# Two graph layers on one core: the x loads, the warm-up, the copies of the opening and ScalarE's order of work are changed

## What is computed

```python
a = adj.astype(x.dtype)
deg = jnp.sum(a, axis=1, keepdims=True)
y = jnp.concatenate([a @ x / deg, x], axis=1) @ weight + bias    # layer 0
x = layernorm(x + y)
h = x @ W.T                                                     # layer 1
e = (h @ a1)[:, None] + (h @ a2)[None, :]
e = jnp.where(adj == 0, -inf, e)
x = layernorm(x + softmax(e, axis=1) @ h)
```

## Time and profile before

| what | value |
|---|---|
| median of 3 runs | 1068.37 us (1066.5 to 1072.28) |
| profiled execution, its own time | 1068.0 us |
| its span, first to last instruction | 1066.3 us |
| mean granted clock of PE | 0.983 of full |
| PE busy | 1002.8 us (94% of the span) |
| ScalarE busy | 598.4 us (56%) |
| VectorE busy | 669.3 us (63%) |
| gathers (q0) | 36864 packets, 268.45 MB, 256 transfers |
| packed store | 1024 KB in each of the first three groups |

### The profile page before, as it was taken

One profiled execution on the slowest core, in us unless ns is written; L12 is line 12 of the kernel. 1 busy time (PEld: TensorE's weight loads), 2 busy tenths in 40 slices (PEclk: granted clock), 3 DMA queues, 4 the chain that ended last, 5 costly groups with the idle time before them and its releaser, 6 DMA issues.

```text
span 1066.3 us, 21633 instructions
## 1 busy us (share of the span) xinstructions
PE 1002.8 (94%) x8769; PEld 873.2 (82%) x8769; DVE 669.3 (63%) x1591; ACT 598.4 (56%) x512; POOL 251.4 (24%) x269
## 2 busy tenths in 40 slices
PE   6787888989899999999999999999999999999996
PEld 6676766878778888888888888888888888888885
DVE  2565667677766867668666675656544656656654
ACT  3887789878788787867767676756421110000000
POOL 2333333333324333333333222222000000000000
PEclk9899988999999999999999999999999999999998
DMA  9799999999999999999999999988330012222011
GB/s 299 283 410 417 423 412 412 410 396 410 407 411 398 419 416 413 397 389 391 386 373 371 359 344 346 338 326 324 122 127 11 32 55 85 85 85 84 16 40 33
DMA packets 51654, 305.33 MB, mean 286 GB/s; under 512 B 6624, under 2 KB 7904, under 8 KB 18016
## 3 DMA queue, kind: packets, MB, share of 16 engines
q0 software_dynamic: 36864, 268.45, 63.7%
q1 hardware_dynamic: 12704, 33.06, 8.8%
q10 hardware_dynamic: 1984, 2.39, 0.8%
HBM read 286.29 MB, written 17.59 MB: 285 GB/s over the span
## 4 chain that ended last, share of the span: by engine, by line
PE 70%; ACT 12%; DMA 9%; issue 5%; DVE 2%; POOL 1%; ACTq 1%; DVEq 0%
PE ps_agg L345 40%; PE ps_part L345 23%; ACT edges L512 9%; DMA adj_in<-in_adj_dram,chunk 8%; PE ps_y L345 4%; DMA bias<-in_L_gnn_bias_dram 1%; DVE edgesT L853 1%; PE ps_h L699 1%; POOL adj_in L1261 1%; ACT L528 1%; ACT L533 1%; PE ps_y L639 1%; ACT edges L542 0%; ACTq L477 0%; PE ps_x1T L692 0%
## 5 line engine op out<-in xcount | busy, mean ns | idle before, releaser
L345 PE MATMUL ps_agg<-parts,edgesT 128*128 128x257 f16 (+1 forms) x5312 | 621.6, 277 | 42.3 <-DVE edgesT L853 42.2
L345 PEld LDWEIGHTS ps_agg<-parts,edgesT 128*128 128x128 fp8e4 x5312 | 523.7, 99 | 128.0 <-DVE edgesT L853 47.6
L512 ACT ACTIVATE edges<-adj_in 128x4096 fp8e4<-128x4096 int32 x126 | 454.6, 3609 | 33.6 <-DMA adj_in<-in_adj_dram,chunk 33.5
L1261 POOL DMA_INDIRECT adj_in<-in_adj_dram,chunk x256 | 249.9, 976 | 496.3 <-ACT edges L512 422.7
L853 DVE STREAM_TRANSPOSE edgesT<-edges 128x512 uint32<-128x512 uint32 x256 | 166.8, 689 | 141.8 <-ACT edges L512 137.5
L345 PE MATMUL ps_part<-parts,edgesT 128*128 128x258 f16 x1664 | 194.6, 273 | 0.0
L345 PEld LDWEIGHTS ps_part<-parts,edgesT 128*128 128x128 fp8e4 x1664 | 162.7, 98 | 22.7
L586 ACT ACTIVATE std<-mean_var,eps 128x1 f32<-128x1 f32 x64 | 18.9, 295 | 204.5 <-DVE mean_var L1090 204.5
L882 DVE SCALAR_TENSOR_TENSOR packed<-edgesT,packed 128x2048 uint32<-128x2048 uint32 x48 | 109.5, 2282 | 0.0
L345 PE MATMUL ps_part<-parts,packed 128*128 128x258 f16 x836 | 96.4, 273 | 0.0
L518 ACT ACTIVATE x1T<-ps_x1T 128x128 f32<-128x128 f32 x64 | 17.6, 275 | 138.6 <-PE ps_x1T L692 138.6
(11 more groups left out here) (116 smaller groups left out, 595.1 us busy)
## 6 DMA issues: line engine op xcount, KB each, us to landing
adj_in<-in_adj_dram,chunk POOLq DMA_INDIRECT x256, 9.0
out_dram<-edges SPq DMA_DIRECT2D x60, 64.0 KB, 2.9
partial_sums<-partial SPq DMA_DIRECT2D x13, 258.0 KB, 7.3
adj_in<-partial_sums SPq DMA_DIRECT2D x13, 258.0 KB, 6.0
packed_adj<-packed SPq DMA_DIRECT2D x3, 1024.0 KB, 9.3
adj_in<-packed_adj SPq DMA_DIRECT2D x2, 1024.0 KB, 6.6
x_all<-in_x_dram SPq DMA_DIRECT2D x6, 256.0 KB, 8.7
x_all<-in_x_dram ACTq DMA_DIRECT2D x6, 256.0 KB, 10.3
```

The source lines that it names most:

```text
L345: done = eng.matmul(bank[:, 0:cols], rows[:, n // BYTES, n % BYTES, :], moving[:, n, :], start=(n == first), stop=(n == last))
L512: act.activation(edges[:, half, :, :], adj_in[:, n % SLOTS, :, :], ACT.Copy, scale=EDGE[t % GROUP], saturate=False).then_inc(s_conv, 1)
L1261: pool.indirect_dma_start(adj_in[:, n % SLOTS, r, :], None, adj_chunks, bass.IndirectOffsetOnAxis(chunk[:, 0:1], 0), element_offset=first_ ...
```

## The change

- GpSimd makes the identity first, then issues the loads of x's partitions 64 to 127 (with their own semaphores `s_xp`), then the chunk numbers; the gathers no longer wait for x. SyncE's queue gets the bias, w1 and a2 behind its x loads. ScalarE's queue keeps only the first piece of x and w0.
- PE transposes the identity into `ps_small` six times before group 0 and eight times before group 1 (`WARM`).
- VectorE copies the transposed x of odd groups (`copy_odd_xT`), ScalarE that of even ones; the four first conversions come after steps 10, 12, 14 and 16.
- `late_group(t)` is t + 1 for t = 1 to 14.
- In ScalarE's step, `convert(t + 1, 0)` comes first, then the late copy, then the x1T copy.

```diff
-        FIRST_AFTER = [11, 13, 15, 16]
+        FIRST_AFTER = [10, 12, 14, 16]
+        WARM = [6, 8]
...
-            j = (t + 3) // 2
-            return j if t % 2 == 1 and AHEAD <= j < GROUPS else None
+            return t + 1 if AHEAD <= t + 1 < GROUPS else None
...
+            sp.dma_start(bias[:, :], b0.rearrange("(o f) -> o f", o=1).to_broadcast([P, F])).then_inc(s_bias, 16)
+            sp.dma_start(w1_sb[:, :], w1).then_inc(s_const1, 16)
+            sp.dma_start(a2_sb[:, :], a1[F:2 * F].rearrange("(p o) -> p o", o=1)).then_inc(s_const1, 16)
...
-            for s in range(QUARTERS):
-                for a in (2, 3):
-                    first = 1 if s == 0 else 0
-                    act.dma_start(x_all[QUAD * a:QUAD * (a + 1), QBLK * s + BYTES * first:QBLK * (s + 1), :]
-                                  .rearrange("p (b c) f -> p b (c f)", c=BYTES), x_quarters[s, a][:, first:, :])\
-                        .then_inc(s_x[s], 16)
...
-            def copy_xT(j):
+            def copy_even_xT(j):
                 act.wait_ge(s_xT, j + 1)
-                if 0 <= j - 2 < AHEAD:
-                    act.wait_ge(s_v, j - 1)
                 wait(act, s_u, j - 1)
-                act.activation(xT[:, j % 2, :, :].rearrange("p c i -> p (c i)"), ps_xT[j % 2][:, :], ACT.Copy)\
-                    .then_inc(s_xTc, 1)
+                if j == 2:
+                    act.wait_ge(s_v, 1)
+                act.activation(xT[:, 0, :, :].rearrange("p c i -> p (c i)"), ps_xT[0][:, :], ACT.Copy)\
+                    .then_inc(s_xTc[0], 1)
...
             for t in range(TILES + 3):
+                if on(t + 1, 0):
+                    convert(t + 1, 0)
+                if late_group(t) is not None:
+                    copy_late_xT(late_group(t))
                 if on(t, 3):
                     copy_x1T(t - 3)
-                if late_group(t) is not None:
-                    copy_late_xT(late_group(t))
                 for g in range(GROUPS - 1):
                     if t == weighted_at(g):
                         weighted_hi(g)
-                if on(t + 1, 0):
-                    convert(t + 1, 0)
...
-                    pe.wait_ge(s_x[j // QUARTERS], 16 * NQ)
-                wait(pe, s_xTc, j - 1)
+                    pe.wait_ge(s_x[j // QUARTERS], 16 * 2)
+                    pe.wait_ge(s_xp[j // QUARTERS], 16 * 2)
+                wait(pe, s_xTc[j % 2], j // 2)
...
+                for _ in range(WARM[j] if j < len(WARM) else 0):
+                    pe.transpose(ps_small[:, 0:P], ident[:, :], ident[:, :])
...
+            def copy_odd_xT(j):
+                dve.wait_ge(s_xT, j + 1)
+                wait(dve, s_u, j - 1)
+                if j == 3:
+                    dve.wait_ge(s_v, 2)
+                dve.tensor_copy(xT[:, 1, :, :].rearrange("p c i -> p (c i)"), ps_xT[1][:, :]).then_inc(s_xTc[1], 1)
...
             for j in range(GROUPS + 1):
+                if j < GROUPS and j % 2 == 1:
+                    copy_odd_xT(j)
                 if j > 0:
                     split_u_lo(j - 1)
...
+            for s in range(QUARTERS):
+                for a in (2, 3):
+                    first = 1 if s == 0 else 0
+                    pool.dma_start(x_all[QUAD * a:QUAD * (a + 1), QBLK * s + BYTES * first:QBLK * (s + 1), :]
+                                   .rearrange("p (b c) f -> p b (c f)", c=BYTES), x_quarters[s, a][:, first:, :])\
+                        .then_inc(s_xp[s], 16)
...
-            pool.wait_ge(s_x[2], 16 * NQ)
             for n in range(2 * TILES):
                 load_half(n)
```

More of the change, by code:

```diff
@@ L199, in bass_two_graph_layers @@
         g_banks = [ps_agg[1], ps_small]
-        s_x = [sem(f"x_landed{s}") for s in range(QUARTERS)]
+        s_x = [sem(f"x_upper_landed{s}") for s in range(QUARTERS)]
+        s_xp = [sem(f"x_lower_landed{s}") for s in range(QUARTERS)]
         s_xfirst = sem("x_first_words_landed")
@@ L233, in bass_two_graph_layers @@
         s_xT = sem("xT_done")
-        s_xTc = sem("xT_copied")
+        s_xTc = [sem("even_xT_copied"), sem("odd_xT_copied")]
         s_u = sem("u_done")
@@ L546, in _ @@
             for j in range(GROUPS + 1):
-                if j < GROUPS:
-                    copy_xT(j)
+                if j < GROUPS and j % 2 == 0:
+                    copy_even_xT(j)
                 if j > 0:
@@ L635, in dense @@
             def dense(j):
-                pe.wait_ge(s_xTc, j + 1)
+                pe.wait_ge(s_xTc[j % 2], j // 2 + 1)
                 wait(pe, s_lo0, j - 1)
@@ L1244, in _ @@
         def _(pool):
[L1245 to L1248, removed]
             pool.memset(ident[:, :], 0.0).then_inc(s_id, 1)
@@ L1255, in _ @@
                                pattern=[[-1, P]], channel_multiplier=1).then_inc(s_fill, 1)
+            for s in range(QUARTERS):
[4 more added lines that the diff above has]
+                        .then_inc(s_xp[s], 16)
+            for a in range(NQ):
+                pool.iota(chunk[QUAD * a:QUAD * (a + 1), :], pattern=[[0, 1]], base=a,
+                          channel_multiplier=NQ * BYTES).then_inc(s_chunk, 1)
+                pool.wait_ge(s_chunk, a + 1)
             def load_half(n):
```

## The result

| | before | after |
|---|---|---|
| median | 1068.37 us | 1076.12 us |
| lowest to highest | 1066.5 to 1072.28 (7 runs) | 1073.72 to 1079.84 (7 runs) |
| ratio | | 1.007, 95% interval 1.0051 to 1.0089 |
| profiled execution, own time | 1068.0 us | 1074.5 us |
| its span | 1066.3 us | 1072.6 us |

The account below looks back on a forecast made before the run. The gather stream was taken to bound the kernel until about 447 us, then PE's fixed work. Savings of 1.4 + 2.2 + 0.75 + 4 = 8.4 us gave 1059.6 profiled, 1060.0 median; range 1052.5 to 1068 us.

Parts of the forecast that it names:

- The reading of the bound: Whole kernel: the gather stream sets the time until about 447 us (tile 37); after it a fixed amount of PE work follows.
- the forecast 4: Main stage: conversion first in ScalarE's step releases gather slots sooner, saving 4 us of at most 9.4.
- rival 2: Main stage: the gather stream keeps its early speed to the end, saving 9.4 us there; 1054.6 us in all; chance 0.20.
- Rival 1: Main stage: DMA engines are full whatever ScalarE does, so only the opening counts; 1064 us; chance 0.22.
- The zeros for v in tiles 1 to 14 and for the warm-up: Main stage and opening: moved v work and PE's warm-up transposes each change the time by 0; warm-up ends +2.7 and −2.7.
- Step (d): Tile 1: conversion ahead of the late copy releases gather half 7 at about 52 instead of 59.07 us; −0.75 us.
- Step (a): Opening: bias on SyncE's queue lands at about 16 us, group 3's product starts at 18.6; −1.4 us, bounds −2.9 and +1.1.
- Rival 3: Opening gives nothing: bias lands at 18.5 us beside gathers, or the clock falls; 1064 or 1068 us; chance 0.13.
- Step (c): Opening: ungated gathers start near 12.5 us behind GpSimd's x transfers; nothing of this on the path, so 0.
- Step (b): Opening: odd copies hide on VectorE and conversions start earlier, first to fourth taking 11.5 us; −2.2 us, ends −1.3 and −3.
- Rival 4: Opening: slow x transfers on GpSimd delay the gathers; at 4.3 us each, about 1074 us; chance 0.07.

## Why the prediction was wrong

**What held.** The reading of the bound held: with tile 37 6.3 us later, the span is 6.3 us longer, and in every profiled execution the span ends 619.3 to 620.0 us behind the start of tile 37. The slow stretches of the stream did come from late releases; tiles 5 to 37 took 6.8 us less, between the forecast 4 and the 9.4 of rival 2, and the new order alone gave 6.0. Rival 1 (the DMA engines are full whatever ScalarE does) is out: at the same share of 1.01 the stream went from 403 to 417 GB/s. The zeros for v in tiles 1 to 14 and for the warm-up held.

**What only looks as if it held.** Step (d), priced at 0.75, seems to measure 0.76 (tile 0 to tile 5, 53.0 against 52.24). But the same order on the kernel before gave 53.3, and the kernels without it lie between 52.6 and 53.1. The match is luck; no run shows a gain there.

**Step (a) failed, and it is the step that turned the sign.** I let the bias land at 16 with 18.5 as the upper end, "as now, since ungated gathers share the engines". It landed at 25.7; the 2.5 us that I added for VectorE's work behind it were right (25.82 to 28.36). The upper end was not a bound: 18.5 was measured with gathers that started at 15.76, and the change itself had moved them ahead. The sum for (a) was −1.4; it measured +8.3. PE fell to the lower level during the 10.35 us of waiting, which costs about 1.6 us more up to the first conversion (an estimate: with the copies on ScalarE it took 11.16 us from group 3 to there, and 9.57 with the bias early as well). Rival 3 named the gathers beside the bias, but gave the bias's pieces of 512 bytes as the reason and took its old landing as the price. More than the bias was late: the transfers of 256 KB ahead of it in the queue were 7 us late too.

**Step (c) failed in its working and fed (a).** I took 1.24 us for each x transfer from GpSimd, by the gather's row. Eight took 4.62 us, 0.58 each, so the gathers started at 7.55, not at 12.5, with the bias, w1 and a2 issued at most 2 us before and SyncE's last x transfer, issued at 5.1, still to land. I had set 0 on both sides because "nothing of this is on the path", and looked only at what waits for the gathers, not at what shares the engines with them. Gating them again gave 4.8 us (ratios) to 6.5 us (medians) back, ungating the kernel before cost 23.

**Step (b) failed.** −2.2 was forecast; from group 3's product to the end of the fourth conversion it measured +5.5, of which 1.6 are the clock's (by the estimate above). I wrote that the odd copy hides on VectorE, from busy time: 2.07 us in 2.66. The order of its queue was left out: at steps 10, 12, 14 and 16 the transposes of tile 0's quarters stand ahead of the next odd copy and wait for the end of a conversion, and elsewhere the copy follows a split that waits for ScalarE. With all copies on ScalarE this way took 3.5 us less. The rest, 0.5 us, is the new FIRST_AFTER (with the bias early and all copies on ScalarE the way takes 23.9 us, before 23.4): the stretch of four conversions takes 14.3 us even then, not 11.5, and the first conversion came only one step (1.3 us) earlier. The 11.5 counted what ScalarE issues (by its own terms 11.2) and left out that PE waits for the copies behind a conversion and ScalarE then for PE. The trace of before had the price: 35.16 − 31.03 = 4.13 us for two steps with a conversion.

**Other sums.** The 9.4 us of rival 2 are 9.8 by their own terms (251.5 − 244 = 7.5, and 2.3); this changes nothing above.

**Rival 4**, the slower side, had the wrong mechanism: GpSimd's transfers were faster than I assumed, and that made the loss larger. The chance of slower was 0.07, and should have held the case in which a small transfer that is waited for falls behind the gathers.

**What stays open.** The late bias is shown to come from the gathers' traffic, by gating and by ungating. The size of pieces was not varied. That 256 KB of x in pieces of 2 KB were as late as the bias, and that 0.5 KB took as long as 64 KB at the end of the queue, speaks against the small size as the reason; how the engines share their time between the queues was not shown. Nothing faster than 1061 us was found. The five kernels near that time all start tile 37 between 439.7 and 441.4, and in their profiled executions the last start that had to wait is tile 29 (twice), 33, 34 or 37, where it was 37 before. From there PE's own work sets the time, so with the new order a still faster stream could gain only up to about tile 29 to 34.

## What to carry to other kernels

Before a stream of large transfers is let go earlier, list every transfer that will then be in flight beside it and who waits for it; put the small ones that are waited for ahead of the bulk and ahead of their own queue, and do not take their old landing times as bounds. An operation moved to an engine with idle time is hidden only if nothing ahead of it in that engine's queue waits: count the order, not the busy share. Count a loop that crosses two engines from a round of it in the trace, not from one engine's issues. A change of many parts whose gain lies in one (here the place of one conversion in ScalarE's step) should be tried part by part.

## What the runs showed of the hardware

- A broadcast of 64 KB in pieces of 512 bytes, issued at 5.6 to 6.9 us, landed 11.6, 20.2 or 30.7 us after its issue, with the first gather at 15.76, 7.55 or 2.89 us. From issue to landing the DMA share was 1.00 to 1.04 on average. The last 256 KB of x ahead of it in its queue were as late: 0.2, 2.7 and 0.4 us before it.
- Equal shares of 1.01 went with 403 and with 417 GB/s, so a full share does not mean that the stream cannot go faster.
- GpSimd issued plain transfers of 192 to 256 KB in 0.58 us each, and one indirect gather of 1 MB in 0.94 with 0.30 between two.
- PE idle for 2.84 us came back at the lower level in one execution (2.05 us for eight passes), while an idle time of 0.85 us at the same place in the kernel before did not. In the kernel after, the granted clock fell to 0.50 in 10.35 us of idle time.
